# Flamingo gated block on one core: the first batches' transfers in another order, and idle matmuls in three waits

## What is computed

```python
x = x + tanh(g_xattn) * attention(layernorm(x), ctx, ctx)     # q, k, v, o projections with biases
n = layernorm(x)
shared = silu(n @ ws1) * (n @ ws3) @ ws2
routed = sum over the best two experts of softmax(n @ w_router) * expert(n)
x = x + tanh(g_ffn) * (shared / 3 + routed * 2 / 3)
```

## Time and profile before

| | us |
|---|---|
| median of 3 runs | 804.16 |
| lowest and highest | 798.36, 805.25 |
| profiled execution, device time | 805.26 |
| its span, first to last instruction | 803.4 |

### The profile page before, as it was taken

How to read it: one execution, slowest core, us unless ns; L and a number is a source line. 1 busy time by engine, 2 the same in 40 slices (tenths; PEclk the granted TensorE clock), 3 DMA queues, 4 the chain that set the end, 5 groups by cost and what they waited for, 6 DMA issues and landing times.

```text
span 803.4 us, 19358 instructions
## 1 busy us (share of the span) xinstructions
PE 770.1 (96%) x6939; PEld 688.8 (86%) x6940; DVE 527.6 (66%) x1108; ACT 425.8 (53%) x717; POOL 428.1 (53%) x498
## 2 busy tenths in 40 slices
PE   4879999999999998899999999999999999999998
PEld 4656777777777776579999999999999999999998
DVE  5757788889888888757665444444444444446897
ACT  5757777777777877662435333333343343343232
POOL 5634446776666654457672666466746584236000
PEclk9879999999999999889999999999999999999999
DMA  6764556776666554243354646444533422228622
GB/s 211 235 213 159 185 186 222 242 240 214 212 218 213 199 185 147 88 164 119 132 141 124 173 143 175 140 131 116 163 87 85 124 53 72 60 60 316 226 91 80
DMA packets 130689, 127.36 MB, mean 159 GB/s; under 512 B 55232, under 2 KB 113088, under 8 KB 130624
## 3 DMA queue, kind: packets, MB, share of 16 engines
q1 hardware_dynamic: 117008, 82.44, 34.8%
q0 software_dynamic: 13616, 44.08, 15.7%
HBM read 75.32 MB, written 50.91 MB: 157 GB/s over the span
## 4 chain that ended last, share of the span: by engine, by line
PE 66%; DMA 9%; POOL 8%; DVE 6%; issue 6%; ACT 2%; SPq 1%; POOLq 1%; ACTq 0%; DVEq 0%
PE bank L585 8%; PE bank L670 7%; PE bank L586 7%; PE bank L587 7%; PE bank_ss L639 5%; PE bank_sm L654 4%; PE bank_sm L585 4%; PE bank_ss L585 4%; PE bank_sm L586 4%; PE bank_sm L587 4%; PE bank_ss L587 4%; DMA y_d<-y_s,y_rows 4%; PE bank_ss L586 4%; POOL w_l L1689 3%; PE bank L677 3%
## 5 line engine op out<-in xcount | busy, mean ns | idle before, releaser
L1302 DVE TENSOR_REDUCE row_max<-bank_sm 128x4 f32<-128x1024 f32 x124 | 151.7, 1223 | 46.0 <-PE bank_sm L654 45.1
L987 ACT ACTIVATE probs_T<-bank_ss 128x1024 f32<-128x1024 f32 x123 | 126.6, 1029 | 21.8 <-PE bank_ss L639 20.4
L1279 DVE TENSOR_TENSOR gT_l<-gg,gT_h 128x1024 fp32r<-128x1024 f32 x49 | 66.8, 1363 | 105.7 <-ACT gT_h L1136 105.7
L585 PE MATMUL bank_ss<-xg_h,w_h 128*128 128x256 f32 x400 | 113.2, 283 | 0.5 <-DVE gg L1488 0.5
L585 PE MATMUL bank_sm<-xg_h,w_h 128*128 128x256 f32 x400 | 113.5, 284 | 0.0
L585 PE MATMUL bank<-w_h,gT_h 128*128 128x256 f32 x392 | 111.2, 284 | 1.8 <-DVE gT_l L1279 1.8
L587 PE MATMUL bank_ss<-xg_l,w_h 128*128 128x256 f32 x400 | 112.9, 282 | 0.0
L586 PE MATMUL bank_sm<-xg_h,w_l 128*128 128x256 f32 x400 | 112.9, 282 | 0.0
L587 PE MATMUL bank_sm<-xg_l,w_h 128*128 128x256 f32 x400 | 112.9, 282 | 0.0
L586 PE MATMUL bank_ss<-xg_h,w_l 128*128 128x256 f32 x400 | 112.9, 282 | 0.0
L586 PE MATMUL bank<-w_h,gT_l 128*128 128x256 f32 x392 | 110.8, 283 | 0.0
(11 more groups left out here) (208 smaller groups left out, 1940.3 us busy)
## 6 DMA issues: line engine op xcount, KB each, us to landing
qk_d<-qk_s SPq DMA_DIRECT2D x64, 256.0 KB, 2.3
w_raw<-wall POOLq DMA_DIRECT2D x27, 512.0 KB
k<-qk_d SPq DMA_DIRECT2D x48, 256.0 KB
q<-qk_d SPq DMA_DIRECT2D x48, 256.0 KB
xq<-xs_d SPq DMA_DIRECT2D x140, 64.0 KB
y_pairs<-y_d POOLq DMA_DIRECT2D x16, 512.0 KB, 9.9
xs_d<-zero_rows SPq DMA_DIRECT2D x8, 514.0 KB
x<-x SPq DMA_DIRECT2D x16, 256.0 KB, 5.1
```

The costliest lines, as they stand in the source:

```text
L585: pe.matmul(out, ah, bh, start=first and k == 0, stop=False)
L987: act.activation(pT[:, 2 * (pv % 4):2 * (pv % 4) + 2, :].rearrange("p h t -> p (h t)"), exp_bank(V.b, pv)[:, :], ACT.Exp, scale=D ** -0.5) ...
L1279: return v.tensor_tensor(dst, ps, high.bitcast(F32), ALU.subtract)
L1302: v.tensor_reduce(mx[B.slot][:, :, :].rearrange("p t (q r) -> p r t q", r=2)[:, :, :, p], max_bank(B.b, p)[:, :].rearrange("p (r t k) -> p ...
```

## The change

Five edits:
- SP's order for batches 0 to 4: the stores of q of batch 0 go ahead of the load of context 2; the load of x 3 goes behind the copies of q of batch 0; the stores of q of batch 1 go ahead of the copies of its k; the load of context 3 goes behind those copies; the stores of k of batch 2 and the first rows of maxima go ahead of the load of x 4.
- `keep_warm` ahead of the scores of batch 0: seven matmuls, not four.
- seven `keep_warm` matmuls in round -2, place 2, ahead of the transposes of batch 1's normalized rows.
- a new helper `keep_late`: eight matmuls of 256 columns into T2, once ahead of round 15's first scores (behind a wait for the router positions of batch 11) and once behind them.
- DVE's statistics of batch 3 from ahead of place 0's row maximum in round -1 to behind place 1's, and their variance behind place 2's.

```diff
@@ SP, before the rounds
             load_x(b2)
             half_out(b0, 1)
             terms_in(b0, 1)
+            half_out(b0, 0)
             load_c(b2)
-            half_out(b0, 0)
+            terms_in(b0, 0)
             load_x(Batch(3))
-            terms_in(b0, 0)
             half_out(b1, 1)
+            half_out(b1, 0)
+            terms_in(b1, 1)
             load_c(Batch(3))
-            terms_in(b1, 1)
-            half_out(b1, 0)
+            terms_in(b1, 0)
+            half_out(b2, 1)
+            first_rows(0)
             load_x(Batch(4))
-            terms_in(b1, 0)
-            first_rows(0)
-            half_out(b2, 1)
             half_out(b2, 0)
             first_rows(1)
             terms_in(b2, 1)
@@ PE
+            def keep_late(n):
+
+                for k in range(n):
+                    pe.matmul(T2[:, 0:2 * P], counters[:, 0, :], counters[:, :, :].rearrange("p n q -> p (n q)"), start=True, stop=True)
+
@@ PE, one(i)
                     V, pv = late_pair(C, S, p)
+                    if i == NB - 1 and p == 0:
+                        pe.wait_ge(pos_ok, NB - AHEAD)
+                        keep_late(8)
                     if V:
                         scores_to_exp(V, pv)
+                    if i == NB - 1 and p == 0:
+                        keep_late(8)
                     if B and among_first(B, 1) and p == 0:
-                        keep_warm(SS[:, 0:512], 4)
+                        keep_warm(SS[:, 0:512], 7)
...
+                    if p == 2 and A and A.b == 1:
+                        keep_warm(SS[:, 0:512], 7)
                     if p == 2 and A:
                         pe.wait_ge(xn_ok, A.n(1, 1))
@@ DVE, one(i)
-                    if p == 0 and Eb and Eb.b == R:
-                        stats_ahead()
-                        variance_ahead()
...
+                    if p == 1 and Eb and Eb.b == R:
+                        stats_ahead()
+                    if p == 2 and Eb and Eb.b == R:
                         variance_ahead()
```

More of the change, by code:

```diff
@@ L1424, in behind @@
                     if p == 1 and Eb and Eb.b != R:
+                        variance_ahead()
+                    if p == 1 and Eb and Eb.b == R:
+                        stats_ahead()
+                    if p == 2 and Eb and Eb.b == R:
                         variance_ahead()
```

## The result

The changed kernel takes 799.66 us (median of 20 runs, 797.41 to 804.29), the kernel before 803.37 beside it (20 runs, 798.36 to 807.13). The ratio is 0.9968, with a 95% interval of 0.9952 to 0.9983: faster by 0.3%, where 0.9% was forecast against the median known then.

A forecast was written before the change was run, and what follows sets the result against it. The prediction took TensorE to bound the kernel, and transfers the ramp. From the profiled 805.26 us it took 4.5 for the ramp and 4.0 for round 15: 796.8, about 797 us, range 791 to 803.

The forecast's parts named there:

- What bounds the kernel: Whole kernel: TensorE, busy 96% of the span, bounds it; only time it stood or ran at the lower clock can return.
- Batch 0's q: Ramp: moving two loads behind brings batch 0's scores from 28.54 to about 26.8 us, taken as 1.7 us (0.5 to 1.8).
- Batch 1's q: Ramp: with its store sent first, the last copy lands at 37.4 us, not 42.09, a gain of 4.7 us.
- What is late next: Ramp: DVE's maxima limit next, DVE waits 1 us for x 4; first scores for an exponential at 42.8 to 43.2 us.
- the whole ramp: Gain up to the first scores for an exponential: 4.5 us, between 1.5 us lost and 9.3 gained.
- second rival: Ramp: the clock gains, the loads don't; context 3 and x 4 become late, round 0 begins no earlier: 801 us, chance 0.11.
- The ramp's idle matmuls: Round -2 and ahead of batch 0's scores: cost 0, end low-clock stretches beside the transfers' path, worth 0, at most 0.7 us.
- third rival: Loads and clock both gain, and the ramp stays at full clock too: 793 us, chance 0.18.
- Round 15: Fillers in two 1.04 us idles keep the clock up; the stretch ends at 342.1, not 346.1 us: 4.0 us (0 to 4.7).
- first rival: The loads gain, the clock doesn't: it falls in spite of the idle matmuls, about 0.5 us overrun: 801 us, chance 0.20.
- DVE's statistics: Batch 3's moved statistics and variance add 1.3 us to DVE's row of maxima in the ramp, nothing else.

The follow-up runs named there:

- order alone: SP's new order and DVE's moved statistics, no idle matmul added, against the kernel before: 798.46 us beside 799.23, ratio 0.9977 (0.9958 to 0.9996).
- f2_hold_b0: The changed kernel, with SP waiting until all copies of batch 0 have landed before it sends x 3 and batch 1's stores: 800.66 us, one execution.

## Why the prediction was right in sign and wrong in size

**What bounds the kernel**: right, but for a slip: the clock line of the earlier trace rows has two slices at 8 behind the ramp, 17 and 18 of 40, not one. TensorE is still busy for 96%, and from the last exponential to the end it takes 448 to 450 us in every profile. Nothing behind the rounds had a date of its own.

**Batch 0's q, 1.7 us**: too large. 0.47 us between the first two profiles; over all of them 28.8 us with the old order (5) and 28.3 with the new (4), 0.5. The store of the high half did leave 0.6 us earlier (17.89, not 18.47) and the copies 1.25, about as worked out. The step that failed is "0.52/320 = 1.6 us", which took the landing for a matter of volume: with everything behind the copies held back, the scores came no earlier; for the last 1.8 us ahead of them first one engine's worth of traffic ran and then none.

**Batch 1's q, 4.7 us**: 2.6 in the two profiles, 0.7 in the means (41.2, 40.5). Three things were off. The 42.09 of the one profile was the latest of five. DVE's last maximum of batch 0 ended at 40.18 us where 38.7 was worked out, mostly since the row began 1.3 us later, and in six profiles the moved variance took another microsecond of it. And the copies were out at 34.74 us (32.85 + 1.89) instead of 33.6 and had landed at 39.5, not 37.4. The store waited for POOL's low half, which was ready some 1.0 us later than before where 0.5 was taken, and the landing behind context 3, which itself took 5.05 us, was 4.7 us where 3.8 was taken. Why it is still 4.2 us with nothing sent behind stays open.

**What is late next**: half right. DVE waited 1.44 us for x 4, where 1 was taken, and its maxima released batch 1's scores in 9 of 13 profiles. But the working stopped at the first exponential, "I take 4.5 us for the whole ramp". Round 0's fourth exponential has ACT's copy of context 4 ahead of it, and its load is queued behind the copies of batch 2 and takes 6.47 us. ACT's wait there takes what comes earlier (0.86 us in the first profile, 3.14 in the second). Stopping there is the step of the sum that failed most. It is the second rival's mechanism, one context further on; it named context 3 and x 4, which stood too (3.85 and 1.44 us), but it was given 0.11. What is left of 4.5 us at the ninth exponential is 1.7 in the two profiles and 0.3 in the means. Context 4 sent 3.7 us sooner (43.56, not 47.23) brings the ninth exponential 1.3 us forward in the mean; that order was not part of the change. Context 4 is not all of it: with it early the time is about 0.6 us better, which can't be told from none, and the low clock around 42 us, which the prediction kept as it was ("at the low clock as before"), costs 1.3 us of the same path. The Trainium skill's "DMA: Bandwidth & Descriptors", section "Rules for kernel authors", says to issue a transfer early and to wait for it late; here the trace agrees, since ACT's wait of 3.14 us is gone with the load sent 3.7 us sooner, though not in the time, where the gain can't be told from none.

**The ramp's idle matmuls, 0**: right. They raise the mean clock (0.9938 alone, against 0.9915 of before beside it) and no gain in speed can be told (0.9992). What they end is the low stretch near 21 us, beside the transfers' path; the one near 29 us comes in spite of them in 7 of 10 profiles, and the one at 42, which is on the path, in 10 of 10. They cost nothing either: 1.77 and 1.76 us inside waits. The third rival (0.18), the ramp at full clock as well, did not come: half of the low stretch at 42 us went in one profile and none of it in the next. It had a footing all the same, as the one profile without that stretch shows (43.82 us for the first scores, 44.58 in the changed kernel). The kernels with and without these idle matmuls measure the same (0.9973 and 0.9968).

**Round 15, 4.0 us**: right where the clock had fallen. The low stretch ended at 346.1 us, the same work now ends at 341.9, and 342.1 was worked out. Both start round 15's scores at the same time (333.29 and 333.27), so all of it is round 15's. Wrong was its use as a mean. In five profiles without fillers the low stretch was 10.2, 10.2, 3.4, 0 and 0 us. From the ninth to the last exponential these took 5.9, 5.6 and 2.9 us more than the two without, an estimate of 2.9 on average; less the 0.6 to 1.7 by which the sixteen's stretch is longer where nothing falls, and less the stretches of round 14, which these sixteen don't prevent. Round 15's alone measured 0.6 us in the medians and 1.2 by the ratio, with an interval from a gain of 2.8 to a loss of 0.4. The prediction said that some executions have no such stretch, and let this weigh in the first rival's chance instead of in the term.

**DVE's statistics, nothing but 1.3 us in DVE's row**: too small in six of 13 profiles. The variance alone took up to 1.19 us there, and the chain of order alone runs over it. They weren't tried alone, so what this costs in time is open.

Sum in the two profiles: the 1.7 us of the ramp are lost again by round 15's first scores, with the low stretch at 314.9 between, and round 15 gives 4.2; 4.05 was measured. In the medians it is 3.7 us in the first set and 1.4 in the other, by the ratios 2.6 and none. So the sign was right in the first measurement and the size was not: of the two terms of the sum the ramp's 4.5 us was 1.7 between the two profiles and 0.3 in the means, and round 15's 4.0 holds for an execution in which the clock had fallen for 10 us and was used for all.

## What to carry to other kernels

When loads are reordered, follow every transfer that is left behind to the first instruction that waits for it, and past the first milestone: the gain is what is left where the last of these waits ends, here one context later than the sum went. Look also for what runs at the lower clock on that path. Take a stretch at the lower clock from several executions before pricing it, and put fillers ahead of the work that follows a gap, not between an instruction and the next that others wait for.

## What the runs showed of the hardware

- With nothing sent behind them, batch 0's copies ended with about one engine's worth of traffic (7% of 16, 14 GB/s, for 1.2 us) and then 0.6 us of none before the scores that wait for them; a fetch of instructions had taken 1.4 us of one engine shortly before (f2_hold_b0, one execution).
- A load of a context took 3.32, 5.05 and 6.47 us to land in the changed kernel, sent behind three, three and six copies. What makes the second longer than the first was not tried.
- Where the clock fell in rounds 14 and 15 differed between executions of one kernel (10.3 us at 335.8 and 3.4 us at 333.4 for the kernel before), in lengths of 3.4 or 10.2 us, and a mean clock that rose by 0.002 with the ramp's idle matmuls left the time as it was (0.9992, 0.9969 to 1.0015).
- The same projection took 2.04 us at a granted clock of 1.00 and 3.38 us at 0.54.
- VectorE's `TENSOR_SCALAR` of 128x2 elements for the variance of batch 3 took 0.17 us in seven profiles of the new order and 0.80 to 1.19 in six.
